# A fused attention and four-expert layer: the 128 x 128 turns of x and of expert 3 taken through a DRAM scratch in five transfers instead of sixteen within SBUF

## The reference, cut to what matters

```python
# x: (16, 512, 128); sixteen groups of 512 tokens of width 128
xn = _layernorm(x)
# attention without softmax, 32 channels; weights folded out of basis and coefficients
queries, keys, values = xn @ q_w, xn @ k_w, xn @ v_w
scores = einsum('btc,bsc->bts', queries, keys) * decay_weights     # causal, falls with distance
att = (scores @ values) @ o_w.T * out_scale
# four experts on every token, the best two of the router's logits mixed
logits = xn @ router_w + router_b + load_balancer
rw, sel = top_k(logits, 2); rw = softmax(rw)
e0 = silu(xn @ sw_w1) * (xn @ sw_w3) @ sw_w2
e1 = gelu(((xn @ me_eq_w ...) @ me_wv ...) @ me_wo ... @ me_c1w + me_c1b) @ me_c2w + me_c2b
h2 = layer_norm(syn + attn); h2 = layer_norm(h2 + relu(h2 @ ce_f1w + b) @ ce_f2w + b)
e2 = h2 @ ce_gen_w + ce_gen_b
e3 = gelu(xn @ ml_w1 + ml_b1) @ ml_w2 + ml_b2
out = x + att + sum(rw * gathered experts)
```

## Time and profile before

| | |
|---|---|
| median of 3 runs | 473.91 us (473.63 to 476.49) |
| the profiled execution | 473.86 us, span 472.1 us |
| busy share of PE / its weight load / DVE / ACT / POOL | 95 / 79 / 86 / 57 / 53 % |
| granted clock of TensorE | full in all 40 slices |
| DMA | 19.34 MB in 87,924 packets, mean 41 GB/s |
| DVE's wait for `xb` | 23.6 us over 15 turns |

### The profile page before, as it was taken

One profiled execution on the slowest core, in us unless ns is written; L12 is line 12 of the kernel. 1 busy time (PEld: TensorE's weight loads), 2 busy tenths in 40 slices (PEclk: granted clock), 3 DMA queues, 4 the chain that ended last, 5 costly groups with the idle time before them and its releaser, 6 DMA issues.

```text
span 472.1 us, 9860 instructions
## 1 busy us (share of the span) xinstructions
PE 450.4 (95%) x2788; PEld 371.0 (79%) x2788; DVE 403.9 (86%) x1327; ACT 270.9 (57%) x534; POOL 250.2 (53%) x366
## 2 busy tenths in 40 slices
PE   5999999999999999999999999999999999999996
PEld 4768888778778778888878878778788878878776
DVE  5788889797997979889897998979889797987896
ACT  4855728366382845828475483836728375582840
POOL 3874817357272664817457272664717357381451
PEclk9999999999999999999999999999999999999999
DMA  7412121121212121121121212111121122111101
GB/s 262 23 19 46 26 56 25 37 43 28 54 25 50 30 42 38 25 54 26 36 43 30 50 26 53 25 40 40 25 53 25 35 46 43 36 26 32 21 0 47
DMA packets 87924, 19.34 MB, mean 41 GB/s; under 512 B 70272, under 2 KB 87392, under 8 KB 87904
## 3 DMA queue, kind: packets, MB, share of 16 engines
q1 hardware_dynamic: 87616, 19.09, 19.9%
q10 hardware_dynamic: 288, 0.01, 0.0%
HBM read 6.80 MB, written 4.19 MB: 23 GB/s over the span
## 4 chain that ended last, share of the span: by engine, by line
issue 45%; POOL 30%; PE 11%; POOLq 9%; ACT 1%; DMA 1%; DVE 1%; SPq 0%; DVEq 0%
POOL hid3l L475 11%; POOL hidl L479 8%; POOLq L441 6%; POOL n L443 5%; POOL xn L443 3%; POOL rstd_u L489 2%; POOLq L435 2%; PE S L1083 2%; PE S L1085 1%; PE S L1084 1%; POOLq L488 1%; DMA W<-weights 1%; PE EX L1023 1%; PE EX L1043 1%; PE S L961 1%
## 5 line engine op out<-in xcount | busy, mean ns | idle before, releaser
L1083 PE MATMUL S<-xh,WH 128*128 128x512 f32 x224 | 97.8, 437 | 0.2 <-DVE gate L798 0.2
L1085 PE MATMUL S<-xh,WL 128*128 128x512 f32 x224 | 88.6, 395 | 0.0
L1084 PE MATMUL S<-xl,WH 128*128 128x512 f32 x224 | 88.3, 394 | 0.0
L475 POOL TENSOR_TENSOR hid3l<-hid,hid3h 128x512 fp32r<-128x512 f32 x64 | 80.3, 1285 | 0.0
L433 POOL TENSOR_TENSOR veps_x<-mv_x,eps 128x4 f32<-128x4 f32 x16 | 3.2, 202 | 143.0 <-DVE mv_x L630 143.0
L1023 PEld LDWEIGHTS EX<-scaled,hid 128*128 128x128 f32 x512 | 58.4, 192 | 8.3 <-issue 8.1
L1023 PE MATMUL EX<-scaled,hid 128*128 128x128 f32 x512 | 60.5, 276 | 3.5 <-DVE hid L802 2.8
L1083 PEld LDWEIGHTS S<-xh,WH 128*128 128x128 f32 x224 | 42.2, 188 | 15.8 <-issue 3.6
L603 ACT ACTIVATE e3T<-S,VEC 128x512 f32<-128x512 f32 x16 | 11.0, 688 | 75.1 <-DVE e3t L894 72.2
L798 DVE SCALAR_TENSOR_TENSOR gate<-th,S 128x512 f32<-128x512 f32 x64 | 43.9, 686 | 9.8 <-ACT th L554 9.1
L1084 PEld LDWEIGHTS S<-xl,WH 128*128 128x128 f32 x224 | 42.3, 189 | 10.1 <-issue 3.6
(11 more groups left out here) (185 smaller groups left out, 1063.9 us busy)
## 6 DMA issues: line engine op xcount, KB each, us to landing
X<-x SPq DMA_DIRECT2D x16, 256.0 KB, 2.9
xb<-xn SPq DMA_DIRECT2D x240, 16.0 KB, 1.8
e3b<-e3T SPq DMA_DIRECT2D x240, 16.0 KB, 1.8
out<-OUT SPq DMA_DIRECT2D x15, 256.0 KB, 2.3
W<-weights SPq DMA_DIRECT2D x1, 768.0 KB, 8.3
W<-weights SPq DMA_DIRECT2D x1, 512.0 KB, 5.9
W<-weights SPq DMA_DIRECT2D x1, 384.5 KB, 6.9
W<-weights SPq DMA_DIRECT2D x1, 384.0 KB, 6.4
```

The lines of the kernel that those rows point to most:

```text
L475: pool.tensor_tensor(hid3l[:, j, :], hid[3][:, j, :], hid3h[:, j, :], ALU.subtract) \
L1083: pe.matmul(bank[:, :], wh, hi, start=True, stop=False)
L1084: pe.matmul(bank[:, :], wh, lo, start=False, stop=False)
L1085: pe.matmul(bank[:, :], wl, hi, start=False, stop=True).then_inc(unit_ready, 1)
```

## The change

`swap` now first stores the whole 128 x 4 x 128 set into a scratch in DRAM (`turning`, one for x, one for expert 3) with one transfer of 256 KB, waits on SP for that transfer to have landed (semaphores `x_kept`, `e3_kept`), and then fetches the set with four transfers, one for each block column j. Each fills 32 partitions of `xb` or `e3b` with 64 KB, read out of DRAM in 512 pieces of 128 bytes. The result in `xb` and `e3b` is the same, and DVE waits for 4 instead of 16 completions. Nothing else is changed: of the engines, only SP's program and the count in two of DVE's waits differ.

```diff
--- before.py
+++ after.py
@@ -76,7 +76,7 @@
 
 B = 32
 BEHIND = NT - 1
-SWAPS = NT * NT
+SWAPS = P // B
 ZEROTH = BEHIND * P - 1
 DIAGONALS = ZEROTH + 1 + 2 * P
 
@@ -227,6 +227,7 @@
         qk_bank = ATT[:, :, :].rearrange("p t n -> p (t n)")
 
 
+        turning = [nc.dram_tensor(f"turning{n}", (P, NT, P), F32, kind="Internal").ap() for n in range(2)]
         w_loaded = [sem(f"w_loaded{n}") for n in range(len(LOADS))]
         vec_loaded = sem("vec_loaded")
         row_loaded = sem("row_loaded")
@@ -254,6 +255,8 @@
         first_root = sem("first_root")
         x_turned = sem("x_turned")
         x_swapped = sem("x_swapped")
+        x_kept = sem("x_kept")
+        e3_kept = sem("e3_kept")
         x_high = sem("x_high")
         x_split = sem("x_split")
         qk_ready = sem("qk_ready")
@@ -363,21 +366,23 @@
                                                                   [diagonals.ap[0], [0, C], [1, BEHIND * P]])) \
                     .then_inc(mask_loaded, DMA_INC)
 
-            def swap(dst, src, done):
-
-                for i in range(P // B):
-                    for j in range(P // B):
-                        sp.dma_start(dst[j * B:(j + 1) * B, :, i * B:(i + 1) * B],
-                                     src[i * B:(i + 1) * B, :, j * B:(j + 1) * B]).then_inc(done, DMA_INC)
+            def swap(g, dst, src, way, kept, done):
+
+                sp.dma_start(way, src[:, :, :]).then_inc(kept, DMA_INC)
+                sp.wait_ge(kept, g.count(DMA_INC, DMA_INC))
+                for j in range(SWAPS):
+                    sp.dma_start(dst[j * B:(j + 1) * B, :, :].rearrange("p t (i q) -> p t i q", q=B),
+                                 bass.AP(way.tensor, way.offset + j * B, [[T, B], [P, NT], [B * T, P // B], [1, B]])) \
+                        .then_inc(done, DMA_INC)
 
             def swap_x(g):
                 sp.wait_ge(x_normed, g.count(NT, NT))
-                swap(xb, xn, x_swapped)
+                swap(g.prev(), xb, xn, turning[0], x_kept, x_swapped)
 
             def swap_e3(g):
                 b = g.bank("e3")
                 sp.wait_ge(released[b], g.uses_before("e3") + 1)
-                swap(e3b, e3T, e3_swapped)
+                swap(g, e3b, e3T, turning[1], e3_kept, e3_swapped)
 
             def store(g):
                 sp.wait_ge(out_ready, g.count(1, 1))
```

## The result

The changed kernel takes **457.01 us** (median of 4 runs, 456.72 to 458.05), the kernel before 473.77 in the runs beside it: ratio 0.964, 95% interval 0.960 to 0.969.

What follows compares the result with a forecast made beforehand. The prediction took a ring of SP's issues and DVE to bound the kernel; 13 turns falling from 367.92 us to 354.8 at 27.29 each save 13.1, so 473.86 - 13.1 = 460.8 us, range 459 to 468.

Steps and rivals of the forecast that it cites:

- The bound: Whole kernel: a closed loop of SP's issues and DVE, 28.39 us, sets the period of 28.30 us a turn.
- The ring of SP's issues and DVE: 23.04 us from `out_ready` over SP's 32 issues to L780, then 5.35 us over DVE back to `out_ready`.
- SP's new chain: From `out_ready` through both stores and the loads to x's last landing: 14.1 us, or 16.5 with loads paced at 1.05 us.
- turn 1 begins with DVE on time: Turn 1, L1194 to L1194, shows PE's own queue: 27.29 us a turn, so 13 later turns save 13.1 us.
- without 0.1 of them in each turn it would be 459.5: Turn 1 still has a few tenths of waiting at its banks; 0.1 less in each turn gives 459.5 us.
- Turns 0 and 1 stay as they are: PE was not held in turns 0 and 1, so they stay unchanged, as do the 36.4 us after 435.72.
- Rival 1: DVE's and PE's meeting at the turn's start keeps 0.35 us in each of 13 turns: 465.4 us; chance 0.15.
- Rival 3: No change: other waits, such as DVE's before L798, fill the slack and keep the period: 469 to 474 us; chance 0.07.
- Rival 2: Short pieces cost SP or the engines 2.4 us a load, ring 31.3 us: about 512 us, slower; chance 0.11.

## Why the prediction was right in its mechanism and short in its size

- **The bound.** Right. The ring of SP's issues and DVE set the period: three issues fewer open it, and twelve further loads close it again where eight don't.
- **SP's new chain.** 14.1 us had been put, 13.6 was measured, with the wait for `x_normed` at 7.07 (7.05). SP's time for a load, 0.60 taken, was 0.64; the landing, 2.9 taken, was 2.5; the engines' time for a piece, between 13 and 33 ns, was 13.
- **"turn 1 begins with DVE on time ... and from L1194 to L1194 it takes 67.80 - 40.51 = 27.29 us".** This is the step that failed, the term for a turn bound by PE: the turn that served as the pattern carried a piece of the very wait that the change removes. DVE was not on time; it had waited 0.74 us for `xb` in turn 0 (one of the 15 waits of the earlier trace rows), POOL's norm of x started 0.81 us behind the transposes of u in place of 0.07, and turn 1 was 0.16 longer by it; another 0.08 it has for standing outside the loop. A turn bound by PE takes 27.05, and 13 x 0.24 is 3.1 us; with 27.05 in its place the sum gives 457.6. I had judged the turn by one meeting, L766, which cost nothing. "without 0.1 of them in each turn it would be 459.5" named the direction and had less than half of the amount; the range's lower end, 459, was built on that guess.
- **"Turns 0 and 1 stay as they are ... and so does what follows 435.72".** Nearly. Between the two profiled executions turn 0 ends 0.22 us earlier, turn 1 is 0.16 shorter and the end, 35.85 for 36.38, 0.53 shorter. Together with 16.3 for the thirteen turns, where 13.1 had been forecast, that makes the 17.2 us of the span. The beginning varies by more than that from one execution to another (the same transposes stand at 43.15 in the kernel with only expert 3 by the scratch, whose profiled execution took 2.9 us more than its median), so only turn 1's share can be told from chance.
- **Rival 1** (something else keeps part of the wait) didn't come: that meeting at the turn's start costs nothing, L1108 starts on time. **Rival 3** neither.
- **Rival 2** (the pieces cost) fell in both of its forms: not SP's time, not the engines'. A piece of 128 bytes took 13 ns of an engine from DRAM as within SBUF. The section "Why small descriptors are slow (HBM only)" of the Trainium skill's page "DMA: Bandwidth & Descriptors" has transfers within SBUF spared a penalty that short pieces pay with DRAM; the trace shows no such difference at this size. Where the issuing sequencer's track is solid, the Trainium skill's page "Perfetto Trace Analysis" (section "What 'DMA-bound' means") has large descriptors matter; here the pieces of the two sets stayed as short as they were, and the number of issues decided: with three fewer, and all but one of the transfers unchanged in form, the gain was there.

## What to carry to other kernels

A queue whose sequencer issues without a gap between two waits is a link of a ring; write the ring down from the event that opens the queue to the one that returns to it, and compare its sum with the period. If they agree, each 0.6 us of issue costs its full length down to the next bound and nothing below it, so work out that bound first: here 1.3 us of 20.6 was all that there was to gain, and either half of the change, or three issues fewer of 32, brought it. For the next bound don't take the shortest turn of the trace as free of stalls; check each engine's meeting in it and the waits of the turn ahead of it, or sum the starts of the bound engine's queue without its gaps.

## What the runs showed of the hardware that wasn't expected

- SP's time for one issue hardly depends on what is moved: 0.60 us for 128 pieces, within SBUF or from DRAM, 0.64 for 512 from DRAM to SBUF, 0.33 to 0.51 for 256 KB in long rows to the scratch (medians of the kernels above).
- From the last issue to DVE's start it takes 3.4 us with twenty loads of 64 KB in a row and 2.9 with sixteen, where a load of 64 KB lands in 2.5 us with four; with sixteen loads of 16 KB it is 2.0.
- In the kernel with sixteen loads for each set, PE stands idle ahead of L1028 for 3.8 us and then runs it slowly, 6.41 us for the 32 matmuls that take 3.7 to 3.8 elsewhere. PE is idle from 299.8 to 303.6 and busy from there on. The granted clock is 1.00 (2.4 GHz) up to 302.0, 0.50, the lower of its two levels (1.2 GHz), from 302.5 to 309.0, and 1.00 again from 309.5. The rows below have it in three longer stretches, the first two of which mix the levels (0.79 and 0.57):

```profile
300.50:303.60 3.10, 0.00 (x0) 0.00 (x0) 2.27 (x5) 0.00 (x0) 0.00 (x0) 0.79 0.33 90
303.60:310.00 6.40, 6.36 (x33) 6.39 (x34) 6.19 (x23) 1.16 (x2) 0.00 (x0) 0.57 0.24 82
310.50:320.00 9.50, 9.50 (x60) 7.67 (x59) 7.64 (x25) 8.04 (x16) 5.83 (x13) 1.00 0.16 24
```

It didn't lengthen the ring in this turn: DVE's way from L785 (301.19) to `out_ready` (306.54) is 5.35 us, as elsewhere.
